# Mamba's two delta projections folded into one matrix on the chip

## What is computed

```python
xm, z = jnp.split(x @ W_in.T, 2, axis=-1)
xc = jax.lax.conv_general_dilated(xm..., conv_w, ...)          # depthwise, 4 taps
xc = jax.nn.silu(xc + conv_b)
dt, Bm, Cm = jnp.split(xc @ W_xproj.T, [R, R + N], axis=-1)
delta = jax.nn.softplus(dt @ W_dt.T + b_dt)
dA = jnp.exp(delta[..., None] * A)
dBx = delta[..., None] * Bm[:, :, None, :] * xc[..., None]
h = dA_t * h + dBx_t                                           # scan over time
y = einsum(h, C_t) + D_skip * xc;  y = y * silu(z);  return y @ W_out.T
```

## Time and profile before

| | |
|---|---|
| median of 3 runs | 1450.84 us (1449.89 to 1450.91) |
| profiled execution | 1445.63 us |
| its span, first to last instruction | 1443.8 us |
| mean granted TensorE clock | 0.892 |
| x-projection starts in groups 0 to 3 | 20.34, 126.26, 282.23, 437.24 us |

### The profile page before, as it was taken

One profiled execution on the slowest core, in us unless ns is written; L12 is line 12 of the kernel. 1 busy time (PEld: TensorE's weight loads), 2 busy tenths in 40 slices (PEclk: granted clock), 3 DMA queues, 4 the chain that ended last, 5 costly groups with the idle time before them and its releaser, 6 DMA issues.

```text
span 1443.8 us, 13324 instructions
## 1 busy us (share of the span) xinstructions
PE 1135.5 (79%) x3910; PEld 570.5 (40%) x3922; DVE 981.0 (68%) x2194; ACT 720.4 (50%) x1376; POOL 615.1 (43%) x426
## 2 busy tenths in 40 slices
PE   4225968877887969678787876968997899999797
PEld 1002323333332323333333533535453465556565
DVE  5965787578866887467657797555645545549787
ACT  7506653476437552442524524435563357756564
POOL 1970787148732965122113574453423122224322
PEclk7557979988899979689898999989998999999898
DMA  6000000000000000200001000000000200000000
GB/s 209 0 0 1 0 1 0 1 0 1 0 1 1 1 0 0 101 0 1 0 1 66 1 1 1 1 1 1 1 1 0 66 0 1 8 1 8 0 9 7
DMA packets 11271, 17.76 MB, mean 12 GB/s; under 512 B 1304, under 2 KB 7584, under 8 KB 10688
## 3 DMA queue, kind: packets, MB, share of 16 engines
q1 hardware_dynamic: 11200, 16.93, 3.5%
HBM read 15.88 MB, written 1.05 MB: 12 GB/s over the span
## 4 chain that ended last, share of the span: by engine, by line
PE 39%; DVE 12%; ACT 5%; issue 3%; POOL 2%; POOLq 0%; DVEq 0%; ACTq 0%
PE bankE L1840 6%; PE bankE L1225 3%; PE bankS L1803 2%; PE bankE L1757 2%; PE bankS L1788 2%; PE bankS L1757 2%; PE bankE L1287 2%; PE bankE L620 1%; PE bankS L1760 1%; PE bankE L1246 1%; PE bankE L1760 1%; PE bankS L1730 1%; PE bankE L579 1%; PE bankE L1275 1%; PE bankE L613 1%
## 5 line engine op out<-in xcount | busy, mean ns | idle before, releaser
L732 DVE TENSOR_TENSOR_SCAN hs<-dA,carry,bankS 128x512 f32<-128x512 f32 x128 | 156.7, 1266 | 3.1
L332 POOL TENSOR_TENSOR hc<-hs,cb 128x1024 f32<-128x1024 f32 x56 | 131.8, 2353 | 46.3 <-DVE hs L732 43.4
L307 POOL TENSOR_TENSOR cv<-cv,hc 128x1024 f32<-128x1024 f32 x56 | 132.6, 2368 | 4.4
L1715 ACT ACTIVATE c_h<-bankE,C 128x512 f32<-128x512 f32 x144 | 98.7, 687 | 53.1 <-PE bankE L1840 50.7
L1609 POOL TENSOR_TENSOR c_acc<-c_acc,c_tw 128x512 f32<-128x512 f32 x32 | 45.9, 1434 | 159.6 <-DVE c_tw L1934 159.5
L443 ACT ACTIVATE sg<-bankE,C 128x512 f32<-128x512 f32 x80 | 54.8, 687 | 97.2 <-PE bankE L579 96.9
L724 DVE TENSOR_TENSOR bankS<-dx,bankS 128x1024 f32<-128x1024 f32 x64 | 78.3, 1224 | 6.5 <-PE bankS L508 5.9
L1840 PE MATMUL bankE<-c_fH,c_w1H 128*128 128x512 f32 x144 | 81.3, 565 | 1.1 <-ACT c_h L1715 1.1
L393 ACT ACTIVATE dA<-dl,Aneg 128x512 f32<-128x512 f32 x128 | 80.2, 708 | 0.1
L508 PE MATMUL bankS<-bc,sel 96*128 96x512 bf16 x60 | 28.0, 466 | 59.6 <-DVE hs L732 59.6
L542 PE MATMUL bankE<-h2T,wg 128*128 128x512 f32 x128 | 71.2, 639 | 4.0 <-ACT sg L424 1.9
(11 more groups left out here) (523 smaller groups left out, 2899.8 us busy)
## 6 DMA issues: line engine op xcount, KB each, us to landing
c_w<-in_w SPq DMA_DIRECT2D x1, 2304.0 KB, 8.7
X<-in_x SPq DMA_DIRECT2D x4, 256.0 KB, 3.9
wg<-in_gate_T SPq DMA_DIRECT2D x1, 1024.0 KB, 8.0
wu<-in_up_T SPq DMA_DIRECT2D x1, 1024.0 KB, 10.2
f<-in_w SPq DMA_DIRECT2D x1, 1024.0 KB, 7.1
out<-X SPq DMA_DIRECT2D x4, 256.0 KB, 2.3
b_wq<-in_Wqkv SPq DMA_DIRECT2D x1, 768.0 KB, 4.5
g<-in_sw SPq DMA_DIRECT2D x2, 256.0 KB, 3.5
```

Of the source, the lines that this page charges most:

```text
L307: pool.tensor_tensor(cv[:, :, :], cv[:, :, :], (hv if by_vector(i, k) else hc)[:, :, :], ALU.add).then_inc(s["y_acc"], 1)
L332: pool.tensor_tensor(dst[:, :, :], hs[:, k % HS, :, :], cb[:, k % 2, :].unsqueeze(1).to_broadcast([P, HV, G]), ALU.mult).then_inc(s["hc_re ...
L732: V.tensor_tensor_scan(hs[:, k % HS, h, :], dA[:, (HV * k + q) % DA, :], dbx[:, h, :], carry[:, k, h:h + 1], ALU.mult, ALU.add).then_inc(s ...
L1715: act.activation(h[:, n % 3, :], E[k % 2][:, :], ACT.Gelu_apprx_tanh, bias=col("b1_3", k)).then_inc(s["fs_ready"], 1)
```

## The change

W_xproj's first 64 rows and W_dt are multiplied once, in piece F0 of group 0: two products into S[3] (256 x 256, as two halves of 128 rows), and one copy by ScalarE to a new tile `wf`. Their operand `wxr` is a further load, into the last slot of `dA`. In F3 TensorE now makes, for each half h of `xc`: the B/C product (32 columns of `wx`), then the two pre-activation products into S[0] and S[2], accumulated over h. F8 has no TensorE part, and `dtT` is gone. B and C lie in rows 0 to 31 of S[1]. ScalarE's copies of the middle part move: `bct` between the two softplus, `bc3[32:64]` behind both.

```diff
-    wx = sb("wx", [P, HV, R + 2 * NS])
+    wx = sb("wx", [P, HV, 2 * NS])
...
-    dtT = sb("dtT", [R, G])
+    wf = sb("wf", [P, HV, ED])
...
+    wxr = dA[0:R, DA - 1, 0:ED]
...
-        for dst, src in ((wi[:, :], dram["W_inT"]), (wx[:, :, :], dram["W_xT"].rearrange("(h p) n -> p h n", p=P)), (wdt[:, :], dram["W_dtT"]),
+        for dst, src in ((wi[:, :], dram["W_inT"]), (wx[:, :, :], dram["W_bcT"].rearrange("(h p) n -> p h n", p=P)), (wdt[:, :], dram["W_dtT"]), (wxr, dram["W_xR"]),
                          (wo[:, :, :], dram["W_outT"].rearrange("(h p) n -> p h n", p=P))):
...
                     act.activation(zs[:, h, :], S[h][:, :], ACT.Silu).then_inc(s["z_ready"], 1)
+                if i == 0:
+                    act.wait_ge(s["wf_made"], 1)
+                    act.activation(wf[:, :, :].rearrange("p h n -> p (h n)"), S[3][:, :], ACT.Copy).then_inc(s["wf_ready"], 1)
...
                 at_least(act, s["dbc_ready"], i, 1, 1)
-                act.activation(dtT[:, :], S[1][0:R, :], ACT.Copy).then_inc(s["dt_ready"], 1)
-                act.activation(bc3[0:32, :], S[1][R:R + 2 * NS, :], ACT.Copy).then_inc(s["bc_high"], 1)
-                at_least(act, s["bc_rest"], i, 1, 1)
-                act.activation(bct[:, :], bcr[:, :], ACT.Copy).then_inc(s["bc_mid"], 1)
-                act.activation(bc3[32:64, :], bcr[:, :], ACT.Copy).then_inc(s["bc_mid"], 1)
+                act.activation(bc3[0:32, :], S[1][0:2 * NS, :], ACT.Copy).then_inc(s["bc_high"], 1)
             elif p == "F8":
                 for h in range(HV):
                     at_least(act, s["pre_ready"], i, HV, h + 1)
                     at_least(act, s["dx_ready"], i, HV)
                     act.activation(dl[:, h, :], S[2 * h][:, :], ACT.Softplus, bias=col("b_dt", h)).then_inc(s["delta_ready"], 1)
+                    if h == 0:
+                        at_least(act, s["bc_rest"], i, 1, 1)
+                        act.activation(bct[:, :], bcr[:, :], ACT.Copy).then_inc(s["bc_mid"], 1)
+                act.activation(bc3[32:64, :], bcr[:, :], ACT.Copy).then_inc(s["bc_mid"], 1)
...
                 if i == 0:
-                    pe.wait_ge(s["ld_s"], 64)
+                    pe.wait_ge(s["ld_s"], 80)
...
                 pe.matmul(S[1][:, :], wi[:, 3 * P:4 * P], hT[:, :], start=True, stop=True).then_inc(s["inproj"], 1)
+                if i == 0:
+                    for h in range(HV):
+                        mm = pe.matmul(S[3][:, h * ED:(h + 1) * ED], wxr[:, h * P:(h + 1) * P], wdt[:, :], start=True, stop=True)
+                    mm.then_inc(s["wf_made"], 1)
             elif p == "F3":
                 at_least(pe, s["proj_kept"], i, HV, HV)
                 at_least(pe, s["z_ready"], i, HV, HV)
+                if i == 0:
+                    pe.wait_ge(s["wf_ready"], 1)
                 for h in range(HV):
                     at_least(pe, s["xc_ready"], i, HV, h + 1)
-                    mm = pe.matmul(S[1][0:R + 2 * NS, :], wx[:, h, :], xc[:, h, :], start=(h == 0), stop=(h == HV - 1))
-                mm.then_inc(s["dbc_ready"], 1)
-            elif p == "F8":
-                at_least(pe, s["dt_ready"], i, 1, 1)
-                for h in range(HV):
-                    pe.matmul(S[2 * h][:, :], wdt[:, h * P:(h + 1) * P], dtT[:, :], start=True, stop=True).then_inc(s["pre_ready"], 1)
+                    mm = pe.matmul(S[1][0:2 * NS, :], wx[:, h, :], xc[:, h, :], start=(h == 0), stop=(h == HV - 1))
+                    if h == HV - 1:
+                        mm.then_inc(s["dbc_ready"], 1)
+                    for q in range(HV):
+                        mm = pe.matmul(S[2 * q][:, :], wf[:, h, q * P:(q + 1) * P], xc[:, h, :], start=(h == 0), stop=(h == HV - 1))
+                        if h == HV - 1:
+                            mm.then_inc(s["pre_ready"], 1)
...
-                V.tensor_tensor(bcr[:, :], S[1][R:R + 2 * NS, :], bc3[0:32, :], ALU.subtract).then_inc(s["bc_rest"], 1)
+                V.tensor_tensor(bcr[:, :], S[1][0:2 * NS, :], bc3[0:32, :], ALU.subtract).then_inc(s["bc_rest"], 1)
```

More of the change, by code:

```diff
@@ L2216 @@
         "x": d["L0_attn_x"], "cst": _packed(d),
-        "W_inT": d["L0_attn_W_in"].T, "W_xT": d["L0_attn_W_xproj"].T, "W_dtT": d["L0_attn_W_dt"].T, "W_outT": d["L0_attn_W_out"].T,
+        "W_inT": d["L0_attn_W_in"].T, "W_bcT": d["L0_attn_W_xproj"][R:].T, "W_xR": d["L0_attn_W_xproj"][:R], "W_dtT": d["L0_attn_W_dt"].T, "W_outT": d["L0_attn_W_out"].T,
         "W_rT": d["L0_attn_W_router"].T, "gate_T": d["L0_attn_gate_w"].reshape(-1, D).T, "up_T": d["L0_attn_up_w"].reshape(-1, D).T,
```

## The result

The changed kernel has a median of 1452.92 us over 22 runs, the kernel before, beside it, 1450.55. The ratio is 1.0022 (95% interval 1.0013 to 1.0030), so it is 1.9 to 4.4 us slower. A second set of runs gave 1.0014 (1.0002 to 1.0025), 2.0 us. Forecast were 6.3 us, slower: the direction held and the median is at the low end of the range, but the forecast size was two to three times what came.

What follows compares the result with a forecast made beforehand. Hand-overs between engine queues run in program order were taken to bound the kernel. Group delays of 2.5 + 0.35 + 1.45 + 2.0 = 6.3 us, added to 1450.84, gave 1457.1 us, range 1452.0 to 1462.0.

Steps and rivals of the forecast that it cites:

- The stage: From the first B/C product to the first `dbx` in each group: forecast late by 2.5, 0.35, 1.45 and 2.0 us.
- 3.65 us for B and C to be complete: TensorE's new run: B and C complete after 8 instructions, 3.65 us from the start, where they took 1.93 before.
- 0.43 each: TensorE's f32 products: each further instruction takes 0.43 us at full clock, the narrowed 32-column product included.
- The lower bound of 0.85: Group 0 with TensorE's clock full throughout: first `dbx` at 29.65 for 28.80, 0.85 us late.
- The middle value: Group 0 with the clock falling, then rising midway in the nine remaining instructions: `dbx` near 31.3, 2.5 us late.
- The set-up: Group 0's weight products, their copy and the extra load run while engines are idle or with time to spare: no cost.
- rival 4: Set-up: the copy of the product or the load is waited for, at most 0.6 to 1 us more; no chance given.
- The step that failed: Behind the first scan: all queues meet, so the groups' whole 6.3 us delay was let stay to the end.
- Rival 1: Groups hand over through ScalarE, late by only 0.35 to 0.7 us: 2.6 us or less, 1451 to 1453.5; chance 0.22.
- Rival 2: The run of 12 products holds TensorE's clock full behind the stage: 7.7 us gained, 3.1 net, 1447.7; chance 0.07.
- Rival 3: Group 0 at half clock throughout and later clock rises behind groups 1 to 3: 11.5 us slower, 1462.3; chance 0.10.

Runs made afterwards that it cites:

- s: The changed kernel with VectorE's last subtraction of the B/C split queued behind both `dx`; ratio to the kernel before 1.0002 (0.9993 to 1.0010).
- w: The kernel before, products unchanged, with the change's ScalarE copy order and two further copies ahead of the last in each group; ratio to before 1.0014.
- r: The changed kernel with both B/C products ahead of the pre-activation products and ScalarE's old copy order; ratios to the kernel before 0.9997 and 0.9985 in two sets.
- y: The kernel before with three more ScalarE copies (1.9 us) ahead of the last copy in group 3 alone; ratio to before 1.0003 (0.9995 to 1.0011).

## Why the stage was foreseen and the end was not

**The stage: right.** Copies behind both softplus, L714 behind the copies, `dx` and the router behind L714: foreseen, and shown by s, which takes the queueing away and with it 2.8 us of the stage of groups 2 and 3. Forecast and measured, late at the first `dbx`: group 1 0.35 and 0.58, group 2 1.45 and 1.58, group 3 2.0 and 2.2. Each is 0.1 to 0.2 short; one reason is seen in group 2: 3.65 us for B and C to be complete was 3.9 (283.27 to 287.18), since the run of six instructions takes 2.87 us (283.27 to 286.14) for the 2.58 that 0.43 each makes. The six of L478 in the earlier trace rows take 2.68 to the start of the next product (274.87 to 277.55). What changes within the new run, and not in theirs, is the width of the stationary operand, 32 and 128, and the tile that is written; which of them costs the 0.19 us was not tried. Group 0, forecast 2.5 with 0.85 and 4.3 as bounds: 1.05 between the two first traces, of which only one had the fall; paired by the clock, 9.50 less 7.33 and 11.14 less 8.69, it is 2.2 to 2.5. The lower bound of 0.85 had the changed kernel at full clock and before as traced, with a fall; at full clock on both sides it would have been 2.0. The middle value was right in size by some luck: the changed kernel's second trace has the fall and the rise as worked out (half from 21.6 to 25.0 us, `dbx` at 31.40 for 31.3), its first has no fall in the stage at all, and the middle value set the one against a single trace of before, where group 0 as it was took 7.33 to 9.72 us. The sum so paired is 6.6 us, and group 0's part of it is uncertain by about 1 us.

**The set-up, and rival 4:** hidden, as worked out.

**The step that failed** is one sentence of the sum: "Behind the first scan all queues meet, so I let it stay to the end." It passes the whole of 6.3 us on. The stage was about 6.6 us late and the time grew by 3.2 and 2.0 us, so 3.4 to 4.6 us came back outside the stage. The traces can place only a part of that.

They place 1.3 to 1.8 us between group 1's first `dbx` and group 2's first product (138.2 to 138.3 us in the four traces with the products of the change and a late stage, 139.5 to 140.0 in four of before), where the fall of the clock near 226 us is gone. The tail behind group 3 would hold the rest, 995.5 us against 998.5, but that difference goes with the set of runs as much as with the kernel, and before's first trace has 995.1. So the step was wrong by 3.4 to 4.6 us, 1.3 to 1.8 of them are seen where they come back, and for the rest place and cause stay open.

Is it the clock? Within one kernel time and clock go together: of the changed kernel's first 22 those with a granted clock of 0.892 or 0.893 take 1450.1 to 1451.8 us, those with 0.889 or 0.890 take 1452.7 to 1458.5. Between kernels they don't: over the runs of a set the mean granted clock is 0.886 for before, 0.891 for the changed kernel and 0.887 for w, which is as much slower. Both traces of the changed kernel are of its faster half (1450.94 and 1452.68 us, where five of 22 runs took over 1456), so what the slow ones meet was not seen. Why a late stage should meet fewer slow stretches, and r, an early one, more, stays open.

**The rivals.** Rival 1, absorption, gave about the right time for a wrong reason: it had ScalarE take up the delay within groups 2 and 3, and there the first `dbx` is 1.58 and 2.2 us late. Its price, 2.6 us, is nearer to the result than the forecast. Rival 2 had the clock as the place of the gain, held full by the run of 12 products. One fall behind group 1 is gone, 1.3 to 1.8 us; the run alone isn't what does it, since r has it and keeps the fall, and what came back in all was 3.4 to 4.6 us and not 7.7. Rival 3 didn't occur in the two traces.

**A profile that was taken for the typical one.** The profiled execution had a time of 1445.63 us and the median of the runs was 5.2 above it. I carried the difference over as if it were a constant. It was a sign that this execution was not a usual one: the three later traces of before have spans of 1447.4 to 1448.8 us for 1443.8.

The Trainium skill (TensorE: Matmul & The Clock Gate, "What's actually happening") says that the gate's window is free-running and that the point of the transition varies for that reason. The traces agree that the point varies: in group 0 the same kernel took 7.33 or 8.69 us. No run here shows by itself why the mean over many runs should give some of a delay back.

## What to carry to other kernels

Before a copy or a split is put behind other work on one engine, look at who waits for it, and at what stands behind that wait in the other engine's queue: here `dx` could have gone up to 2 us before a subtraction that it didn't need. When a product replaces a chain of two, issue first the part with the longest chain behind it; B and C first gave the shorter stage. Where the profiled execution is some us faster than the median, compare several traces of the same kernel outside the changed place before a sum of a few us is carried to the end.

## What the runs showed that was not expected

- The kernel before against itself: spans of 1443.8, 1447.4, 1447.7 and 1448.8 us, with groups 1 to 3 of the stage equal to 0.02 us. The 3.6 to 5 us lie in group 0, in the stretch from it to group 1 (0.8 to 1.1) and, for the most part, behind group 3: 995.1 us or 998.5. Ahead of group 3 the same products vary by more than these four show: y, not edited there, reaches it at 441.57 us, they at 437.24 to 438.71.
- One copy of 0.65 us more in each group, 2.6 us in sum, moved the time by -0.3 us (-1.6 to +0.9, from the interval 0.9989 to 1.0006); 5.2 us in each group, 19.9 in the stage, moved it by 13.9.
- A fall of the clock can pass from ahead of the stage into it: in w from 264 to 268 us to 282 to 286. A stage sum and what is outside of it then shift by 1.6 us against each other.
- Six f32 instructions with stationary operands of 32 and 128 columns in turn took 2.87 us to the start of the next, where six with 128 columns throughout took 2.68.
